# Cross attention in a decoder kernel: variance step moved to ScalarE, rotary sine product in one VectorE instruction

## The reference, cut to what matters

```python
def _rms_norm(x, w):
    v = mean(square(x), axis=-1, keepdims=True)
    return w * (x * rsqrt(v + 1e-6))
def _rotate_half(x):
    x1, x2 = split(x, 2, axis=-1)
    return concatenate((-x2, x1), axis=-1)
def _rope(x, pos):
    emb = concatenate((pos * inv_freq, pos * inv_freq), axis=-1)   # 128 wide
    return x * cos(emb) + _rotate_half(x) * sin(emb)
kv_in = concatenate([context_hidden, draft_hidden], axis=1)
q = _rope(_rms_norm(draft_hidden @ Wq.T, q_norm_w), draft_pos)
k = _rope(_rms_norm(kv_in @ Wk.T, k_norm_w), all_pos)
v = kv_in @ Wv.T
out = softmax(q @ k.T / sqrt(128)) @ v @ Wo.T      # 4 query heads share one k, v
```

## Time and profile before

| | |
|---|---|
| three runs | 1845.1, 1846.55, 1848.43 us |
| profiled execution, its own time | 1841.2 us |
| its span, first to last instruction | 1839.2 us |
| mean granted TensorE clock | 0.940 of full speed |
| PE busy | 1572.6 us (86% of the span) |
| DVE busy | 1398.4 us (76%) |
| POOL busy | 1153.8 us (63%) |
| ACT busy | 759.1 us (41%) |
| `cross_stream`, first to last instruction | 494.7 to 1741.7 us |
| its slot 0 begins | 552.3 us |
| its last unit is transposed | 1640.8 us |

### The profile page before, as it was taken

One profiled execution on the slowest core, in us unless ns is written; L12 is line 12 of the kernel. 1 busy time (PEld: TensorE's weight loads), 2 busy tenths in 40 slices (PEclk: granted clock), 3 DMA queues, 4 the chain that ended last, 5 costly groups with the idle time before them and its releaser, 6 DMA issues. The chain is left out here.

```text
span 1839.2 us, 26261 instructions
## 1 busy us (share of the span) xinstructions
PE 1572.6 (86%) x8370; PEld 892.6 (49%) x8370; DVE 1398.4 (76%) x2944; ACT 759.1 (41%) x1808; POOL 1153.8 (63%) x990
## 2 busy tenths in 40 slices
PE   5586695774378999999999999899999999999787
PEld 4465463532244554555455455455545555554344
DVE  8786447878888778788788877978878787786454
ACT  2253454541535444434444344353534434433252
POOL 3652460121357789777778877776987777776452
PEclk8699797986599999999999999999999999999889
DMA  2000711000500001000000100000000000000010
GB/s 63 1 2 3 266 37 46 3 27 3 190 1 1 1 1 37 1 1 1 1 1 1 36 1 1 1 1 1 1 1 1 1 1 1 1 1 1 17 53 23
DMA packets 27854, 38.23 MB, mean 21 GB/s; under 512 B 4676, under 2 KB 24392, under 8 KB 27464
## 3 DMA queue, kind: packets, MB, share of 16 engines
q1 hardware_dynamic: 27720, 36.57, 5.9%
HBM read 35.51 MB, written 1.05 MB: 20 GB/s over the span
## 5 line engine op out<-in xcount | busy, mean ns | idle before, releaser
L1963 POOL TENSOR_TENSOR stream_acc<-stream_acc,stream_p 128x512 f32<-128x512 f32 x448 | 569.8, 1275 | 214.8 <-ACT stream_p L1886 210.4
L1886 ACT ACTIVATE stream_p<-stream_lowered 128x512 f32<-128x512 f32 (+1 forms) x480 | 302.4, 630 | 680.0 <-DVE stream_lowered L2023 677.0
L1828 PE MATMUL stream_banks<-stream_p,stream_v 128*128 128x512 f32 (+1 forms) x960 | 490.7, 593 | 0.9 <-ACT stream_p L1886 0.9
L2023 DVE TENSOR_TENSOR stream_lowered<-stream_banks,stream_shift_all 128x512 f32<-128x512 f32 (+1 forms) x480 | 329.6, 687 | 188.9 <-PE stream_banks L1815 162.8
L2030 DVE TENSOR_REDUCE stream_tops<-stream_banks 128x1 f32<-128x512 f32 (+1 forms) x512 | 321.2, 629 | 23.8 <-PE stream_banks L1801 23.8
L1801 PE MATMUL stream_banks<-stream_k_t_hi,stream_q_t_hi 128*128 128x512 bf16 (+1 forms) x512 | 184.1, 361 | 25.0 <-DVE stream_tops L2030 23.2
L1828 PEld LDWEIGHTS stream_banks<-stream_p,stream_v 128*128 128x128 f32 (+1 forms) x960 | 175.6, 190 | 57.8 <-ACT stream_p L1886 2.8
L1815 PE MATMUL stream_banks<-stream_q_t_hi,stream_k_t_hi 128*128 128x512 bf16 (+1 forms) x480 | 183.0, 381 | 0.0
L1815 PE MATMUL stream_banks<-stream_q_t_hi,stream_k_t_lo 128*128 128x512 bf16 (+1 forms) x480 | 182.1, 379 | 0.0
L1815 PE MATMUL stream_banks<-stream_q_t_lo,stream_k_t_hi 128*128 128x512 bf16 (+1 forms) x480 | 182.1, 379 | 0.0
L1968 POOL TENSOR_TENSOR stream_by_cos<-stream_by_cos,stream_by_sin 128x512 f32<-128x512 f32 x96 | 120.1, 1251 | 50.1 <-DVE stream_by_sin L2058 49.9
(11 more groups left out here) (397 smaller groups left out, 2968.7 us busy)
## 6 DMA issues: line engine op xcount, KB each, us to landing
memory_raw_t<-in_ctx_t SPq DMA_DIRECT2D x4, 1601.0 KB, 9.7
cross_ctx_t<-in_ctx_t SPq DMA_DIRECT2D x4, 1601.0 KB, 7.2
memory_raw<-in_ctx SPq DMA_DIRECT2D x4, 1536.0 KB
cross_w_raw_q<-in_L_xattn_Wq SPq DMA_DIRECT2D x1, 2048.0 KB, 12.4
cross_w_raw_o<-in_L_xattn_Wo SPq DMA_DIRECT2D x1, 2048.0 KB, 19.7
moe_raw_up<-in_L_ffn_wi SPq DMA_DIRECT2D x8, 256.0 KB, 4.5
model_x<-in_x SPq DMA_DIRECT2D x1, 1024.0 KB, 5.4
ffn_raw_fc<-in_L_ffn_w_fc SPq DMA_DIRECT2D x1, 1024.0 KB, 5.0
```

The source lines that it names most:

```text
L1828: nc.tensor.matmul(ps[:, 2 + n, :], v[0:r, g % 2, t, :], p32[0:r, step % 4, :], start=(t == 0), stop=(t == KT - 1)).then_inc(weighed, 1)
L1886: nc.scalar.activation(p32[0:r, step % 4, :], lowered[0:r, step % 3, :], ACT.Exp, scale=SCALE).then_inc(p32_ready, 1)
L1963: nc.gpsimd.tensor_tensor(acc[0:r, g % 2, cols], acc[0:r, g % 2, cols], p32[0:r, step % 4, :], ALU.add).then_inc(acc_ready, 1)
L2023: nc.vector.tensor_tensor(lowered[0:r, step % 3, :], ps[0:r, step % 2, :], shift_all[0:r, g % 2, n * HALF:(n + 1) * HALF], ALU.add).then_i ...
```

## The change

`var` is made on ACT right behind the squares, by an ACTIVATE with function Identity, scale 1/128 and a bias tile of 1e-6 that POOL sets once. `by_sin` is made by one DVE instruction per part instead of two; the sine table has its halves exchanged, so the product lies with its halves exchanged too, and POOL's `add_up` puts them in place by two instructions of half the width.

```diff
 def half_tables(engine, tab, gain, cos, sin, s):
     cols, n = slice(s * H2, (s + 1) * H2), cos.shape[1]
+    other = slice((1 - s) * H2, (2 - s) * H2)
     engine.tensor_tensor(tab[0][:, :, cols], cos, bcast(gain[:, 0, cols], 1, n), ALU.mult)
-    return engine.tensor_tensor(tab[1][:, :, cols], sin, bcast(gain[:, 1, cols], 1, n), ALU.mult)
+    return engine.tensor_tensor(tab[1][:, :, other], sin, bcast(gain[:, 1, cols], 1, n), ALU.mult)
...
+                def vary(u, n):                                            # ScalarE
+                    heads = slice(0, width(u))
+                    if u == 0:
+                        ac.wait_ge(eps_ready, 1)
+                    else:
+                        ac.wait_ge(rms_ready, max(u - 1, 1))
+                    ac.wait_ge(squared, part_at[(u, n)] + 1)
+                    nc.scalar.activation(var[:, u % 2, heads], ss[:, u % 2, heads], ACT.Identity, bias=eps[:, 0:1],
+                                         scale=1.0 / HD).then_inc(var_ready, 1)
...
                         square(u, 0)
                         if unit(u)[1] >= QT:
                             take_values(u, 0)
+                        else:
+                            vary(u, 0)
                     for u in units_at(slot, 4):
                         if unit(u)[1] >= QT:
                             square(u, 1)
                             take_values(u, 1)
+                            vary(u, 1)
...
             def _(gp):                                                     # GpSimd
                 angle_link = chain(gp, pool_step)
+                nc.gpsimd.memset(eps[:], 1e-6).then_inc(eps_ready, 1)
...
-                    nc.gpsimd.tensor_tensor(by_cos[:, u % 2, 0:n], by_cos[:, u % 2, 0:n], by_sin[:, u % 2, 0:n], ALU.add).then_inc(summed, 1)
+                    for s in range(2):
+                        to, of = slice(s * H2, (s + 1) * H2), slice((1 - s) * H2, (2 - s) * H2)
+                        last = nc.gpsimd.tensor_tensor(by_cos[:, u % 2, 0:n, to], by_cos[:, u % 2, 0:n, to], by_sin[:, u % 2, 0:n, of], ALU.add)
+                    last.then_inc(summed, 1)
...
                     nc.vector.tensor_tensor(by_cos[:, u % 2, some], heads, tab[0], ALU.mult)
-                    for s in range(2):
-                        to, of = slice(s * H2, (s + 1) * H2), slice((1 - s) * H2, (2 - s) * H2)
-                        last = nc.vector.tensor_tensor(by_sin[:, u % 2, some, to], heads[:, :, of], tab[1][:, :, to], ALU.mult)
-                    last.then_inc(taken, 1)
-
-                def vary(u):                                               # VectorE
-                    n = width(u)
-                    if u >= 2:
-                        ve.wait_ge(rms_ready, u - 1)
-                    nc.vector.tensor_scalar(var[:, u % 2, 0:n], ss[:, u % 2, 0:n], 1.0 / HD, 1e-6, ALU.mult, ALU.add).then_inc(var_ready, 1)
+                    nc.vector.tensor_tensor(by_sin[:, u % 2, some], heads, tab[1], ALU.mult).then_inc(taken, 1)
...
                         rotate(u, 0)
-                        if unit(u)[1] < QT:
-                            vary(u)
                     for u in units_at(slot, 6):
                         if unit(u)[1] >= QT:
                             rotate(u, 1)
-                            vary(u)
```

More of the change, by code:

```diff
@@ L1622, in cross_stream @@
         ss = sb("ss", [P, 2, 4])
+        eps = sb("eps", [P, 1])
         var = sb("var", [P, 2, 4])
@@ L1644, in cross_stream @@
         scored, lowered_ready, p32_ready, acc_ready, weighed = (sem(s) for s in ("scored", "lowered_ready", "p32_ready", "acc_ready", "weighed"))
+        eps_ready = sem("eps_ready")
         att_hi, att_lo, out_ready, added = sem("att_hi"), sem("att_lo"), sem("out_ready"), sem("added")
```

## The result

The changed kernel runs in 1824.1 us (median of four runs, 1822.37 to 1826.58) against 1845.82 us before (four runs): ratio 0.9887, 95% interval 0.9873 to 0.9901. Forecast were 1825.3 us, 21.3 us less than before; measured are 21.7 us less. The profiled execution took 1824.63 us with a span of 1822.9 us.

What follows compares the result with a forecast made beforehand. PE was taken as the bound, waiting for late DVE. Savings of 22.6 us less POOL's 0.8 and 0.5 gave -21.3 us, 1846.55 to 1825.3 us; own range 1818 to 1834, 8-in-10 range 1813 to 1838.

Steps and rivals of the forecast that it cites:

- PE is the bound and waits for DVE in slots 9 and 14: Slot 0 to last unit: PE busy 1042.6 of 1088.7 us, waiting 25.4 us in 26 transposes for DVE's `add_out`.
- Slot 9, ordinary groups, 0.91 us, and slot 14, 0.65 us: Savings from both DVE parts: slot 9 of groups 1, 3, 5, 7, 9, 11, 12, 13; slot 14 of thirteen groups.
- `var`'s price is the wait for POOL's running instruction: On DVE, SBUF-only `var` waits out POOL's running instruction: 0.94 us in slot 9 of group 3 against 0.155 shortest.
- Groups 4 and 8: Angle work makes DVE late, so two `var` count by slot 9: 0.97 + 1.13 + 0.12 us each, plus slot 14.
- The term of 0.97 us: Groups 4 and 8, first of two `var` counted between slots 7 and 9: start-to-start distance 876.22 - 875.25.
- the stall moves to the neighbour: Rival: in late slots `add_out` waits POOL out instead of `var`; only 3.4 us won, 1843 us; chance 0.09.
- Group 0: Has the angle work but no `add_out`; one `var` counted as won, 0.97 us, rounded to 1.0.
- Groups 2, 6, 10: Slot 9 there saves only 0.40 us for `var`, 0.46 with the sine; 1.4 us for the three groups.
- The merged sine: One `by_sin` of 128x512 takes 0.60 us instead of 0.66 for two halves; 0.06 saved per part in late places.
- ACT at no cost: `var` on ACT takes 0.25 us in idle time behind the squares in slot 8: cost 0, at worst 1 to 10.
- POOL, +0.8 and +0.5 us: `add_up` in halves adds 0.14 us a unit: 0.8 us lost in a few table-making groups, 0.5 in the lead-in.
- The forecast's 22.6 us in the slots: Sum of both DVE savings: slot 9 7.3, groups 2, 6, 10 1.4, groups 4 and 8 4.4, slot 14 8.5, group 0 1.0.

Runs made afterwards that it cites:

- run 3: Kernel before with `var` still on DVE, but reading a PSUM operand and issued ahead of the two `by_sin` halves: ratio to before 0.9920.
- run 2: Kernel before with only the merged `by_sin` and POOL's sum in halves, `var` staying on DVE: ratio to before 0.9996.
- Run 8: Changed kernel with the clamp, the last angle instruction on DVE, moved ahead of the rotation in its slot: ratio to before 0.9885.
- run 7: Changed kernel with one more ACT copy of 128x512 behind each `var`: ratio to before 0.9905.
- runs 1: Kernel before with only `var` moved to ACT; sine tables, two `by_sin` halves and single `add_up` as before: ratio to before 0.9888.

## Why the prediction was right

- *PE is the bound and waits for DVE in slots 9 and 14.* Right: PE's busy time did not change, its waits for `add_out` fell from 25.4 to 2.9 us.
- *Slot 9, ordinary groups, 0.91 us, and slot 14, 0.65 us.* Right: 74.77 - 73.21 = 1.56 us, their sum. That is 12.5 of the 20.8 us.
- *`var`'s price is the wait for POOL's running instruction.* Right, by run 3 and by the two groups of run 2.
- *Groups 4 and 8.* Wrong in size: 2.87 us each forecast (2.22 in slots 6 and 8, which the forecast counts as 7 to 9, and 0.65 for slot 14), 1.23 measured. By the starts of `lower`, slot 8 fell by 1.20 us and slot 13 by 0.66, as forecast. The term of 0.97 us was counted as won, but the clamp behind it took over the wait. This is the rival "the stall moves to the neighbour", true in this one place: `add_out` reads PSUM and is free of it, the clamp is not. Run 8 shows the 0.98 us. And the 0.65 us of slot 14 was lost again in slot 15, where another engine is the late one: ACT makes the sines, between two table loads. Its first load starts 1.36 us into slot 13 in both kernels (893.98 - 892.62 us before, 888.50 - 887.14 after), and the whole block is as long as before, so what DVE wins inside it is not won. The part of `q_t` that DVE makes behind ACT's, in slot 15 of group 4, before and after:

```profile
900.75 0.69 DVE L2069 TENSOR_TENSOR stream_q_t_lo<-stream_banks,stream_q_t_hi 128x512 bf16<-128x512 f32 x1 [1.48 <-ACT stream_q_t_hi L1914]
```

```profile
895.27 0.69 DVE L2080 TENSOR_TENSOR stream_q_t_lo<-stream_banks,stream_q_t_hi 128x512 bf16<-128x512 f32 x1 [2.13 <-ACT stream_q_t_hi L1927]
```

  DVE waits 0.65 us longer for ACT, and slot 15 grew from 3.37 to 4.03 us. The forecast counted slot 14 in all thirteen groups without looking at what ACT does in these two. Group 0 was forecast at 1.0 us and fell by 0.68; with the clamp early it fell by another 0.55.
- *Groups 2, 6, 10.* 1.11 us each forecast, 1.67, 2.48 and 1.15 measured. Group 10 is as forecast. 1.3 us of group 6's is no gain: in before's profile, and in no other, its 128x512 bfloat16 matmuls took 0.63 us instead of 0.38 for a while. The granted clock of that stretch is the last number but two (other columns as in the earlier trace rows):

```profile
1035.40:1039.40 4.00, 3.87 (x10) 1.79 (x11) 2.93 (x5) 1.63 (x3) 2.96 (x5) 0.57 0.54 220
```

  It is the lower of the two levels (1.2 GHz) for most of the 4 us. PE had waited 1.22 us before it, as it does in slot 9 of groups without such a stretch, so what set it off stays open. The 0.56 us that group 2 won beyond the forecast stay open too.
- *The merged sine.* 26 x 0.06 = 1.6 us forecast, 1.5 us measured (1154.0 to 1152.5), but only because `var` was gone; alone it is worth nothing in an ordinary group. The prediction added the two parts as if each could be won by itself.
- *ACT at no cost.* Right: 0.30 us instead of 0.25, and run 7 shows room for 0.6 more in ordinary groups. The table loads in the stage stayed at four beside the exponents and four beside the sines. The Trainium skill's page "ScalarE: Activation LUTs", section "Rules for kernel authors", would keep such a step on VectorE. By the formula in its section "What ACT_TABLE_LOAD costs" the Trainium skill's estimate for the ACTIVATE is 0.28 us, near the 0.30 measured. What ran beside the step decided here: on VectorE it cost 0.67 us at the median, not 0.155.
- *POOL, +0.8 and +0.5 us.* Two halves cost the forecast +0.14 us a unit (in the lead-in the halves start 0.69 us apart and the next instruction 1.37 us after the first, where it was 1.23 before), but no lost time shows for it; the lead-in as a whole did not grow (58.5 to 58.2 us), and in slot 24 `normed` kept its 0.29 us of room, because POOL had been idle behind `add_up`. The lead-in of runs 1, 3 and 7 was about 2 us longer than in the others; PE's granted clock was 0.93 there against 0.97, but before had 0.93 too, and this stays open.

That the total came out within 0.4 us, 21.7 against 21.3, is in part luck. The forecast's 22.6 us in the slots were 19.5, without the 1.3 us of clock, and the 1.3 us that POOL was to give back did not show. Slots and lead-in together then account for 19.8 of the 21.7 us; the difference is within the interval of the ratio, 18.3 to 23.4 us. The ordinary groups, 12.5 us of the sum, were not luck.

## What to carry to other kernels

An instruction's price on a busy engine is its start-to-start distance in the place where that engine is late, and it can be many times its own work when it waits for another engine; look at the shortest and the longest of its group before the mean. Before counting a removed wait as won, ask whether the instruction that moves into its place has the same kind of operands and would wait the same way. Moving work about within a late stretch of an engine moves the hole; taking work out of the stretch closes it.

## What the runs showed of the hardware

Two forms of VectorE instruction and a GpSimd `tensor_tensor` don't run side by side here: a TENSOR_SCALAR with its only tensor in SBUF (the 128x4 `var`, the 128x960 clamp), and a SCALAR_TENSOR_TENSOR with two tensors in SBUF (the 128x960 angle step, 1.15 or 1.90 us). The one that starts second ends behind the other by its own length less about 0.13 us: `var`, 0.155 us long alone, ended 0.03 us behind POOL's sum, the clamp (0.65) 0.52 us behind it, and POOL's sum (1.26) 1.13 us behind the clamp. VectorE instructions with a PSUM operand ran at their usual length beside the same sums (0.148 us for 128x4, 0.68 us for 128x512).

In the profiles of before, of the change and of runs 2 and 8, `var` or the clamp was issued 128 times behind the start of a POOL instruction that had 0.15 us or more to go, and waited it out 126 times. The two that didn't were issued 0.01 and 0.08 us behind POOL's start; others as close did wait, so near ties can fall either way. In the two groups of run 2 POOL's record starts first by the same 0.01 us. In the kernel before the clamp began at 876.22 and POOL's `add_up` 0.01 us later; the clamp took its 0.65 us, and `add_up` 1.49 us where 1.00 is usual:

```profile
876.23 1.49 POOL L1968 TENSOR_TENSOR stream_by_cos<-stream_by_cos,stream_by_sin 128x384 f32<-128x384 f32 x1
```
